# Layer-1 attention: value columns of four heads as the stationary operand, probabilities moved

## The chip, the core and the metric

The kernel runs on one core of a Trainium2 chip. The metric is the device time of one execution in microseconds. The core has TensorE (PE, with its weight loads shown apart as PEld), VectorE (DVE), ScalarE (ACT), GpSimd (POOL) and SyncE (SP), which here only issues transfers.

## What is computed

Two blocks over x of shape (2, 1024, 256): a cross attention of layer 0, a mixture of experts, a cross attention of layer 1 and a second feed-forward block. The change is in the third step. Its part of the reference:

```python
q = (queries @ Wq.T + bq).reshape(N, L, H, -1)        # N=2, L=1024, H=16 heads of 16
k = (keys @ Wk.T + bk).reshape(N, S, H, -1)           # S=77 context rows
v = (values @ Wv.T + bv).reshape(N, S, H, -1)
sm = jnp.einsum('nlhd,nshd->nlhs', q, k) / math.sqrt(D)
sm = jnp.where(causal_mask[None, :, None, :], -jnp.inf, sm)
sm = jax.nn.softmax(sm, axis=-1)
attn = jnp.einsum('nlhs,nshd->nlhd', sm, v)
return attn.reshape(N, L, H * D) @ Wo.T + bo
```

Only the first 77 tokens of a batch see a mask that cuts anything.

## The kernel before

Layer-1 attention (about 1440 to 1700 us of the profile) runs as a loop over 64 half heads, k = 0 to 63: two batches of 16 heads, and for each head two halves of 512 tokens. Each engine has its own program with its own copy of that loop, and dictionaries such as OUT_T, OUT_P, OUT_LN and R1V say at which k an engine does a side job. The order on an engine is the order in which the code is written; engines wait for one another by semaphores.

- Keys and queries are kept in split precision. Projected queries and keys are stored to DRAM and come back as stacks (QS, KS): for each head 49 rows with high and low parts and one row for the negated row maximum (NM). SP issues them (stack_queries1, stack_max1, stack_keys1). Chunk c = 0 holds heads 0 to 7 and c = 1 heads 8 to 15.
- Before the loop, bound matmuls with block keys KD give each token's maximum (max1); DVE reduces them, PE turns them, DVE negates them into NM, and SP sends them into QS. For the second batch all this happens inside the loop, at k = 17 to 28.
- scores1(k): one 512-column matmul gives 77 x 512 scores, in a PSUM bank of its own (two banks); for the first half one more adds the mask. PE runs it 3 half heads ahead.
- ACT takes the exponential into PT1 (a ring of four). The upper 16 bits of PT1 are the high part; the remainder PR1 is made by POOL, or by DVE where k is in R1V (k = 5, 7, 9, 11, then every fourth up to 31, then all odd ones).
- attend1(k): for each of four tiles of 128 tokens, four products with the tile's probabilities as stationary operand (128 columns) and the head's 16 value columns and a column of ones moved: 16 matmuls of 17 columns.
- norm1(n), on DVE, once per head: reciprocal of the sums (128 x 8) and a multiply (128 x 128) into Y, tokens on partitions.
- When a batch is done, its groups of 512 tokens are turned by PE (out_turn), rounded by ACT (round_out), the rest taken by DVE (rest_out), projected by PE (project_out1, 14 matmuls of 256 columns in each of two parts), added to X by DVE (add_out1) and normalised. Groups 0 and 1 run in the loop between k = 36 and 57, groups 2 and 3 behind it, one after the other. Then the router's matmuls (route) start.

The heart of the product before:

```python
for t in range(4):
    c = slice(t * P, t * P + P)
    mm = product(pv1[n % 2][:, 4 * a + t, :],
                 [(p[0:S, c], V1[v][0:S, b, h, :]) for p in (upper1(k), PR1[:, k % RING1, :]) for v in "hl"])
```

## Time and profile before

| | us |
|---|---|
| median of 3 runs (1809.47 to 1811.34) | 1811.26 |
| the profiled execution | 1816.01 |
| its span | 1814.2 |

| engine | busy us | share |
|---|---|---|
| PE | 1569.1 | 86% |
| PEld | 1287.9 | 71% |
| DVE | 1238.8 | 68% |
| ACT | 706.7 | 39% |
| POOL | 899.0 | 50% |

The mean granted clock of TensorE is 0.898 of full speed. A granted clock of 1.00 is 2.4 GHz and one of 0.50 is 1.2 GHz. A matmul's duration in the rows includes its way through the array and overlaps the next; the distance between two starts is its cost in a dense run. A line of the profile can be that of a helper: L1921 is the matmul inside product(), which attend1, the projections and the router all use.

### The profile page before, as it was taken

What the parts mean: (1) busy time and instruction counts of PE and PEld (TensorE: products, weight loads), DVE (VectorE), ACT (ScalarE), POOL (GpSimd) and SP (SyncE); (2) the same over time, 40 slices, a digit from 0 to 9 for tenths busy, and PEclk for the clock granted to TensorE, in tenths of its full rate; (3) what the DMA queues carried; (4) which work ended last, traced back from release to release, by engine and by line L of the source; (5) the groups of instructions that cost most, each with busy time, mean ns of one, the idle gap of its engine ahead of it and who ended that gap; (6) DMA issues with size and microseconds to landing.
All of it is one profiled execution on the core that took longest, in us unless ns stands there. A gap on an engine that the chain in (4) does not pass through costs nothing.

```text
span 1814.2 us, 44910 instructions
## 1 busy us (share of the span) xinstructions
PE 1569.1 (86%) x18034; PEld 1287.9 (71%) x18034; DVE 1238.8 (68%) x2503; ACT 706.7 (39%) x1312; POOL 899.0 (50%) x862
## 2 busy tenths in 40 slices
PE   1889999999999999999999975399988856898798
PEld 0777788777777778777877763299977834565587
DVE  8757777777777577777777775244488566455765
ACT  1334444444433454444444431155544404232122
POOL 3246555655564356565556651477655506221322
PEclk9899999999999999999999996599999955555699
DMA  9124424443432243344343416477776480600101
GB/s 216 37 62 125 97 71 112 109 105 85 103 96 64 69 100 85 96 108 106 84 106 93 112 37 227 178 260 258 251 243 209 157 137 1 116 3 1 36 12 36
DMA packets 83376, 199.60 MB, mean 110 GB/s; under 512 B 17739, under 2 KB 40835, under 8 KB 82788
## 3 DMA queue, kind: packets, MB, share of 16 engines
q1 hardware_dynamic: 79428, 186.47, 38.5%
q0 software_dynamic: 3744, 10.26, 1.5%
q8 instruction: 146, 2.39, 0.5%
q14 instruction: 58, 0.48, 0.1%
HBM read 104.46 MB, written 39.72 MB: 79 GB/s over the span
## 4 chain that ended last, share of the span: by engine, by line
PE 51%; DVE 20%; POOL 7%; issue 6%; ACT 6%; DMA 5%; DVEq 1%; ACTq 0%; SPq 0%; POOLq 0%
PE ps L1921 20%; PE ps L2020 9%; PE ps L1954 5%; PE ps L2000 5%; PE ps L2001 5%; DMA latf<-wexp 4%; POOL PR L869 3%; DVE PR L1420 3%; ACT hf L1178 2%; POOL wst L881 2%; DVE hf L1606 2%; ACT hs_h L1180 2%; DVE mxs L1354 2%; PE ps L2285 2%; DVE wtmp L1448 1%
## 5 line engine op out<-in xcount | busy, mean ns | idle before, releaser
L869 POOL TENSOR_TENSOR PR<-PT 128x512 f16<-128x512 f32 (+1 forms) x416 | 441.3, 1071 | 423.8 <-ACT PT L1093 423.1
L1093 ACT ACTIVATE PT<-ps 128x512 f32<-128x512 f32 (+1 forms) x576 | 324.1, 597 | 367.3 <-PE ps L2001 367.0
L2020 PE MATMUL ps<-V_h,PT 128*128 128x65 f16 (+1 forms) x2304 | 325.2, 197 | 26.8 <-DVE PR L1420 21.1
L2020 PE MATMUL ps<-V_l,PT 128*128 128x65 f16 (+1 forms) x2304 | 320.5, 195 | 0.0
L2020 PE MATMUL ps<-V_l,PR 128*128 128x65 f16 (+1 forms) x2304 | 318.8, 194 | 0.0
L2020 PE MATMUL ps<-V_h,PR 128*128 128x65 f16 (+1 forms) x2304 | 318.3, 194 | 0.0
L2020 PEld LDWEIGHTS ps<-V_h,PT 128*128 128x128 bf16 (+1 forms) x2304 | 227.0, 99 | 121.9 <-issue 48.2
L1354 DVE TENSOR_REDUCE mxs<-ps 128x1 f32<-128x736 f32 x256 | 235.3, 919 | 48.3 <-PE ps L1954 48.2
L2000 PE MATMUL ps<-QA,KA 128*128 128x512 f32 (+1 forms) x576 | 248.5, 431 | 5.5 <-DMA QB<-maxT 4.9
L2001 PE MATMUL ps<-QB,KB 65*128 65x512 f32 (+1 forms) x576 | 231.8, 402 | 0.0
L2020 PEld LDWEIGHTS ps<-V_l,PT 128*128 128x128 bf16 (+1 forms) x2304 | 228.9, 99 | 0.6
L2020 PEld LDWEIGHTS ps<-V_h,PR 128*128 128x128 f16 (+1 forms) x2304 | 227.7, 99 | 0.0
L2020 PEld LDWEIGHTS ps<-V_l,PR 128*128 128x128 f16 (+1 forms) x2304 | 226.3, 98 | 0.0
L1954 PE MATMUL ps<-KA,QA 128*128 128x368 f32 x768 | 198.3, 349 | 28.8 <-issue 17.5
L1352 DVE TENSOR_REDUCE mxs<-ps 128x1 f32<-128x368 f32 x256 | 137.2, 536 | 53.8 <-PE ps L1954 53.8
L1954 PEld LDWEIGHTS ps<-KA,QA 128*128 128x128 f32 x768 | 126.9, 190 | 48.8 <-issue 23.9
L1420 DVE TENSOR_TENSOR PR<-PT 128x512 f16<-128x512 f32 (+1 forms) x160 | 146.5, 931 | 10.3 <-ACT PT L1093 9.2
L937 POOL TENSOR_TENSOR hs_l<-hf,hs_h 128x512 f16<-128x512 f32 x92 | 110.7, 1208 | 62.4 <-ACT hs_h L1180 61.6
L1921 PE MATMUL ps<-xsp_h,wup 128*128 128x128 f16 x1472 | 132.9, 221 | 2.3 <-DVE xsp_l L1595 2.3
L2193 PE MATMUL ps<-wdn,hs_h 128*128 x736 | 123.8, 273 | 9.0 <-POOL hs_l L937 8.9
L1921 PE MATMUL ps<-xsp_l,wup 128*128 128x128 f16 x736 | 127.7, 221 | 0.0
L2000 PEld LDWEIGHTS ps<-QA,KA 128*128 128x128 f32 (+1 forms) x576 | 108.2, 188 | 26.6 <-issue 8.3
(351 smaller groups left out, 3670.3 us busy)
## 6 DMA issues: line engine op xcount, KB each, us to landing
wup<-wsplit SPq DMA_DIRECT2D x46, 1024.0 KB
QA<-Q_h SPq DMA_DIRECT2D x64, 256.0 KB, 4.6
latf<-wexp SPq DMA_DIRECT2D x32, 512.0 KB, 4.4
wsplit<-wst SPq DMA_DIRECT2D x32, 512.0 KB, 2.9
KA<-K_h SPq DMA_DIRECT2D x32, 275.5 KB, 3.1
KA<-K_l SPq DMA_DIRECT2D x32, 275.5 KB, 4.0
KB<-K_h SPq DMA_DIRECT2D x32, 275.5 KB, 5.4
QB<-Q_l SPq DMA_DIRECT2D x32, 256.0 KB, 5.5
```

The source lines that it names most:

```text
L869: nc.gpsimd.tensor_tensor(PR[0:m, s % RING, :], PT[0:m, s % RING, :], upper(s)[0:m], ALU.subtract).then_inc(s_rem_pool, 1)
L937: nc.gpsimd.tensor_tensor(hs["l"][:, j % 2, cols], hf[:, n % 3, :], hs["h"][:, j % 2, cols], ALU.subtract).then_inc(s_hlo, 1)
L1093: nc.scalar.activation(PT[0:m, s % RING, :], score_banks[s % 2][0:m], ACT.Exp, scale=HD ** -0.5).then_inc(s_exp, 1)
L1352: nc.vector.tensor_reduce(mxs[:, 0, t:t + 1], ps[:, 2, 0:MAXW], AX.X, ALU.max).then_inc(s_mxfree, 1)
L1354: nc.vector.tensor_reduce(mxs[:, 1, t:t + 1], ps[:, pair:pair + 2, 0:MAXW], AX.XY, ALU.max).then_inc(s_mxfree, 1)
L1420: nc.vector.tensor_tensor(PR[0:m, r % RING, :], PT[0:m, r % RING, :], upper(r)[0:m], ALU.subtract).then_inc(s_rem_dve, 1)
L1921: mm = nc.tensor.matmul(o, l, r, start=(k == 0), stop=(k == n - 1), **kw)
L1954: mm = nc.tensor.matmul(ps[:, 2 + i + (2 if two and a == 1 and t % 2 == 1 else 0), 0:MAXW], q, KA[h][:, MAXC[i]:MAXC[i] + MAXW], start=Tru ...
L2000: nc.tensor.matmul(o, KA[h][:, k], QA[h][:, q], start=True, stop=False)
L2001: nc.tensor.matmul(o, KB[h][0:HD + 1, k], QB[h][0:HD + 1, q], start=False, stop=True) \
L2020: mm = nc.tensor.matmul(pv_bank[:, q, :], p, v, start=(kt == 0 and q == 0 and k == 0), stop=(kt == KT - 1 and k == 3), skip_group_check=True)
L2193: mm = nc.tensor.matmul(out_banks[j % 2], hs[a][:, j % 2, f * P:f * P + P], down_weights(j, f // 4, b, slice(f % 4 * D, f % 4 * D + D)), s ...
```

## The change

The product is turned round. Four heads' value columns stand in a stationary operand of 128 columns: for head j of a chunk its 16 values are at columns 16j, ones for its sum are at the columns 64 away, and all else is zero. The probabilities, high part and remainder, are moved, 512 columns at a time, so one half head takes 4 matmuls of 512 columns (values high and low with each). Four heads add into one bank: values on 64 partitions, and each head's sum, replicated 16 times, on the other 64. The order of the half heads becomes: for a chunk and a group of four heads, the four heads of the first half, then the four of the second. norm1 runs once for four half heads, on 64 partitions x 512. Its output has channels on partitions, in Y's memory, so out_turn goes away; one rounding of 128 x 1024 and one remainder replace two each.

Scores, exponentials and remainders now work on all 128 rows: KS is cleared with a memset and its stationary is 128 columns wide. Both value arrays are cleared by POOL, with 16 small fills of ones. Query stacks are sent in quarters, and SP sends the maxima of the first batch before the second chunk's stacks. The output side jobs move: group 2 is now rounded at k = 60 and projected at k = 62 and 63, and only group 3 is projected behind the loop.

```diff
-        score1 = [ps[0:S, 3, :], ps[0:S, 4, :]]
-        pv1 = [ps[:, i, 0:TB * (D1 + 1)].rearrange("p (t d) -> p t d", t=TB) for i in (5, 2)]
+        score1 = [ps[:, 3, :], ps[:, 4, :]]
+        pv1 = [ps[:, 5, :], ps[:, 2, :]]
+        UNIT = 4
+
+        def half_head(k):
+            b, r = divmod(k, K1S // B)
+            u, i = divmod(r, UNIT)
+            c, g, a = u // 4, u // 2 % 2, u % 2
+            return b, c, g, a, i
+
+        def value_rows(g):
+            return slice(HD * g, HD * g + HD)
+
+        def sum_rows(g):
+            return slice(HD * (1 - g), HD * (1 - g) + HD)
+
+        def units_before(g):
+            return 8 * (g // 2) + 7 + g % 2
...
-        OUT_T, OUT_P, OUT_LN, OUT_XT = {36: 0, 43: 1}, {39: 0, 46: 1}, {42: 0, 49: 1}, {50: 0, 56: 1}
+        OUT_T, OUT_P, OUT_LN, OUT_XT = {29: 0, 35: 1, 60: 2}, {32: 0, 38: 1, 62: 2}, {35: 0, 41: 1}, {42: 0, 49: 1}
...
             stack_keys1(0)
-            for c in range(NC):
-                stack_queries1(0, c, 0)
+            for g in range(2):
+                stack_queries1(0, 0, g)
             sp.wait_ge(s_a1e, NM_JOB[0] + 2)
             for c in range(NC):
-                stack_max1(0, c, 0)
+                for g in range(2):
+                    stack_max1(0, c, g)
+            for g in range(2):
+                stack_queries1(0, 1, g)
             stack_keys1(1)
-            sp.wait_ge(s_comb, GR)
             sp.wait_ge(s_a1e, Q_DONE[1] - 1)
             store_queries1(1, 0)
             sp.wait_ge(s_a1e, Q_DONE[1])
             store_queries1(1, 1)
-            for c in range(NC):
-                stack_queries1(1, c, 0)
-            sp.wait_ge(s_sc1, 2 * (HC + 4))
-            for c in range(NC):
-                stack_queries1(1, c, 1)
+            sp.wait_ge(s_sc1, K1S // 4)
+            for g in range(2):
+                stack_queries1(1, 0, g)
             sp.wait_ge(s_a1e, NM_JOB[1] + 2)
-            for i in range(2):
-                for c in range(NC):
-                    stack_max1(1, c, i)
-
-            sp.wait_ge(s_a1e, OUT_JOB + 4 * GR)
+            for g in range(2):
+                stack_max1(1, 0, g)
+            sp.wait_ge(s_sc1, K1S // 2)
+            for g in range(2):
+                stack_max1(1, 1, g)
+            for g in range(2):
+                stack_queries1(1, 1, g)
...
-            nc.gpsimd.memset(V1["h"][:, :, :, D1:D1 + 1], 1.0).then_inc(s_l1c, 1)
-            nc.gpsimd.memset(V1["l"][:, :, :, D1:D1 + 1], 0.0).then_inc(s_l1c, 1)
+            for k in "hl":
+                nc.gpsimd.memset(V1[k][:], 0.0).then_inc(s_l1c, 1)
+            pool.wait_ge(s_l1c, 9)
+            for h in range(H1):
+                col = (D1 * h + HD) % P
+                nc.gpsimd.memset(V1["h"][0:S, :, h, col:col + D1], 1.0).then_inc(s_l1c, 1)
...
+                b, a = divmod(g, 2)
+                act.wait_ge(s_nm1, units_before(g))
+                act.wait_ge(s_a1, OUT_JOB + 2 * g)
+                nc.scalar.copy(A1T["h"], A1f[b][:, :, HALF * a:HALF * a + HALF]).then_inc(s_a1h, 1)
...
+            nc.vector.memset(KS[:].bitcast(F32), 0.0).then_inc(s_ones, 1)
+            dve.wait_ge(s_ones, 3)
             for c in range(NC):
-                nc.vector.memset(KS[HD * c + QM:HD * c + QM + 1].bitcast(F32), 1.0).then_inc(s_ones, 1)
+                nc.vector.memset(KS[HD * c + QM:HD * c + QM + 1, :, :, 0:S].bitcast(F32), 1.0).then_inc(s_ones, 1)
...
             def norm1(n):
-                b, h = divmod(n, H1)
-                dve.wait_ge(s_pv1, 2 * n + 2)
-                nc.vector.reciprocal(rs8[:, n % 2], pv1[n % 2][:, :, D1]).then_inc(s_rs1, 1)
-                dve.wait_ge(s_rs1, n + 1)
-                nc.vector.scalar_tensor_tensor(out=Y[:, TB * b:TB * b + TB, D1 * h:D1 * h + D1],
-                                               in0=pv1[n % 2][:, :, 0:D1], scalar=vs1[:, 1:2],
-                                               in1=rs8[:, n % 2].unsqueeze(2).to_broadcast([P, TB, D1]),
-                                               op0=ALU.mult, op1=ALU.mult).then_inc(s_nm1, 1)
+                b, c, g, a, _ = half_head(UNIT * n)
+                vr, sr, bank = value_rows(g), sum_rows(g), pv1[n % 2]
+                dve.wait_ge(s_pv1, UNIT * (n + 1))
+                link(dve, nc.vector.reciprocal(rec[vr], bank[sr]))
+                nc.vector.scalar_tensor_tensor(out=A1f[b][vr, c, HALF * a:HALF * a + HALF], in0=bank[vr], scalar=vs1[vr, 1:2],
+                                               in1=rec[vr], op0=ALU.mult, op1=ALU.mult).then_inc(s_nm1, 1)
 
             def rest_out(g):
-                for c in range(NC):
-                    rest_job(12 + NC * g + c, A1T["l"][:, c, :], tbank[(OUT_JOB + 4 * g + c) % 2], A1T["h"][:, c, :])
+                b, a = divmod(g, 2)
+                rest_job(12 + g, A1T["l"], A1f[b][:, :, HALF * a:HALF * a + HALF], A1T["h"])
...
-                    for b in range(B):
-                        ins = nc.vector.tensor_scalar(V1["h"][0:S, b, :, 0:D1], V1f[0:S, b], vs1[0:S, 0:1], None, ALU.mult)
+                    def values1(v, j):
+                        return v[0:S].rearrange("p b (c j) d -> p b c j d", c=NC)[:, :, :, j, :]
+
+                    for j in range(HC):
+                        ins = nc.vector.tensor_scalar(values1(V1["h"], j)[:, :, :, D1 * j:D1 * j + D1], values1(V1f, j),
+                                                      vs1[0:S, 0:1], None, ALU.mult)
                     link(dve, ins)
-                    for b in range(B):
-                        nc.vector.scalar_tensor_tensor(out=V1["l"][0:S, b, :, 0:D1], in0=V1f[0:S, b], scalar=vs1[0:S, 0:1],
-                                                       in1=V1["h"][0:S, b, :, 0:D1], op0=ALU.mult, op1=ALU.subtract) \
-                            .then_inc(s_v1, 1)
+                    for j in range(HC):
+                        nc.vector.scalar_tensor_tensor(out=values1(V1["l"], j)[:, :, :, D1 * j:D1 * j + D1], in0=values1(V1f, j),
+                                                       scalar=vs1[0:S, 0:1], in1=values1(V1["h"], j)[:, :, :, D1 * j:D1 * j + D1],
+                                                       op0=ALU.mult, op1=ALU.subtract).then_inc(s_v1, 1)
...
-            norm1(K1S // 2 - 1)
-            for g in range(GR // 2, GR):
-                rest_out(g)
-                for i in range(2):
-                    add_out1(g, i)
-                dve.wait_ge(s_a1e, OUT_JOB + 4 * g + 4)
-                normalise(dve, X, Y, 4 * g, 4, s_xn)
+            norm1(K1S // UNIT - 1)
+            add_out1(GR - 2, 1)
+            rest_out(GR - 1)
+            dve.wait_ge(s_a1e, OUT_JOB + 3 * GR - 2)
+            normalise(dve, X, Y, 4 * (GR - 2), 4, s_xn)
+            for i in range(2):
+                add_out1(GR - 1, i)
+            dve.wait_ge(s_a1e, OUT_JOB + 3 * GR)
+            normalise(dve, X, Y, 4 * (GR - 1), 4, s_xn)
...
             def scores1(k):
-                n, a = divmod(k, 2)
-                b, h = divmod(n, H1)
-                c = h // HC
+                b, c, g, a, i = half_head(k)
                 if k >= 2:
                     pe.wait_ge(s_ex1, k - 1)
-                o, j = score1[k % 2], h % HC
-                if a == 0 and h == 0:
+                if k % (K1S // B) == 0:
                     pe.wait_ge(s_ks[b], 16 * 6)
-                if a == 0 and (h % HC == 0 or (b > 0 and h % HC == 4)):
-                    pe.wait_ge(s_qs[b][c][h % HC // 4], 64)
-                slot = j if b == 0 else (HC + j) % QSLOTS
-                r = slice(HD * c, HD * c + QROWS)
-                mm = nc.tensor.matmul(o, KS[r, b, j, 0:S], QS[r, slot, HALF * a:HALF * a + HALF], start=True, stop=(a == 1))
+                if a == 0 and i == 0:
+                    pe.wait_ge(s_qs[b][c][g], 64)
+                o, j, r = score1[k % 2], 4 * g + i, slice(HD * c, HD * c + QROWS)
+                mm = nc.tensor.matmul(o, KS[r, b, j, :], QS[r, j, HALF * a:HALF * a + HALF], start=True, stop=(a == 1))
                 if a == 0:
-                    mm = nc.tensor.matmul(o[:, 0:P], ident_r[0:S, 0:S], mask[0:S, 1, :], start=False, stop=True)
+                    mm = nc.tensor.matmul(o[:, 0:P], ident_r[0:S, :], mask[0:S, :], start=False, stop=True)
                 mm.then_inc(s_sc1, 1)
 
             def attend1(k):
-                n, a = divmod(k, 2)
-                b, h = divmod(n, H1)
-                if a == 0 and n >= 2:
+                n = k // UNIT
+                b, c, g, a, i = half_head(k)
+                if i == 0 and n >= 2:
                     pe.wait_ge(s_nm1, n - 1)
                 if k in R1V:
                     pe.wait_ge(s_r1v, R1V.index(k) + 1)
                 else:
                     pe.wait_ge(s_r1p, k + 1 - sum(v <= k for v in R1V))
-                for t in range(4):
-                    c = slice(t * P, t * P + P)
-                    mm = product(pv1[n % 2][:, 4 * a + t, :],
-                                 [(p[0:S, c], V1[v][0:S, b, h, :]) for p in (upper1(k), PR1[:, k % RING1, :]) for v in "hl"])
+                h = HC * c + 4 * g + i
+                for m, (v, p) in enumerate((v, p) for v in "hl" for p in (upper1(k), PR1[:, k % RING1, :])):
+                    mm = nc.tensor.matmul(pv1[n % 2], V1[v][:, b, h, :], p, start=(i == 0 and m == 0),
+                                          stop=(i == UNIT - 1 and m == 3))
                 mm.then_inc(s_pv1, 1)
-
-            def out_turn(g):
-
-                pe.wait_ge(s_nm1, H1 * (g // 2 + 1))
-                for c in range(NC):
-                    bk = job(OUT_JOB + 4 * g + c)
-                    for t in range(4):
-                        mm = nc.tensor.transpose(bk[:, t * P:t * P + P], Y[:, 4 * g + t, c * P:c * P + P], ident[:])
...
-                if k in OUT_T:
-                    out_turn(OUT_T[k])
                 for i in range(2):
                     if k - i in OUT_P:
                         project_out1(OUT_P[k - i], i)
                 if k in OUT_XT:
                     transposes(2, OUT_XT[k])
-            for g in range(GR // 2, GR):
-                out_turn(g)
-                for i in range(2):
-                    project_out1(g, i)
-            for g in range(GR // 2, GR):
-                transposes(2, g)
-
-
-            pe.wait_ge(s_a1e, OUT_JOB + 4 * GR)
+            transposes(2, GR - 2)
+            for i in range(2):
+                project_out1(GR - 1, i)
+            transposes(2, GR - 1)
```

## Rows read from the trace of the kernel before

**Rows 1.** Page: busy sums, and granted TensorE clock in 40 slices

```profile
PE 1569.1 (86%) x18034; PEld 1287.9 (71%) x18034; DVE 1238.8 (68%) x2503; ACT 706.7 (39%) x1312; POOL 899.0 (50%) x862
...
PEclk9899999999999999999999996599999955555699
```

**Rows 2.** Busy us (count) per engine, granted clock, DMA share, GB/s

```profile
1520.00:1530.00 10.00, 4.86 (x61) 3.81 (x60) 8.97 (x24) 3.68 (x7) 6.93 (x7) 0.50 0.00 1
...
1550.00:1560.00 10.00, 9.23 (x68) 6.53 (x68) 3.61 (x7) 2.56 (x4) 1.05 (x2) 0.66 0.26 105
...
1640.00:1650.00 10.00, 10.00 (x116) 6.59 (x114) 7.64 (x17) 5.10 (x9) 3.40 (x4) 0.50 0.01 2
1700.00:1710.00 10.00, 9.33 (x44) 4.63 (x43) 10.00 (x15) 3.87 (x6) 7.91 (x3) 0.82 0.00 0
```

**Rows 3.** PE in order of time, two steps: start us, us, operation

```profile
1501.97 0.71 PE L2285 MATMUL ps<-QS,KS 49*77 49x512 f32 x1
1502.61 0.20 PE L1921 MATMUL ps<-V_h,PT 77*128 77x17 f16 x1
...
1503.14 0.71 PE L2285 MATMUL ps<-QS,KS 49*77 49x512 f32 x1
...
1504.54 0.71 PE L2285 MATMUL ps<-QS,KS 49*77 49x512 f32 x1
```

**Rows 4.** PE in order of time, 512-column f32r matmuls at either clock

```profile
1545.26 0.63 PE L1921 MATMUL ps<-XT_l,wa_h 128*128 128x512 f32 x1
1545.69 0.63 PE L1921 MATMUL ps<-XT_h,wa_l 128*128 128x512 f32 x1
...
1711.18 0.40 PE L1921 MATMUL ps<-XT_h,diag_l 128*128 128x512 f32 x1
1711.42 0.39 PE L1921 MATMUL ps<-XT_l,diag_h 128*128 128x512 f32 x1
```

**Rows 5.** DVE groups by shape, 1490 to 1720: busy us, mean ns, idle before

```profile
L1725 DVE SCALAR_TENSOR_TENSOR Y<-ps,vs,rs 128x128 f32<-128x128 f32 x32 | 11.2, 351 | 1.1
...
L1723 DVE RECIPROCAL rs<-ps 128x8 f32<-128x8 f32 x32 | 6.5, 204 | 33.6 <-PE ps L1921 33.3
...
L1661 DVE SCALAR_TENSOR_TENSOR A<-ps,bqk,Q_h 128x512 fp32r<-128x512 f32 x4 | 3.0, 744 | 2.4 <-ACT Q_h L1144 2.4
...
L1852 DVE RECIPROCAL logits<-logits 128x128 f32<-128x128 f32 x1 | 1.0, 953 | 0.0
```

**Rows 6.** DVE's remainders, line 1801: duration ns min/median/max

```profile
L1801 DVE TENSOR_TENSOR PR<-PT x25: 676/1187/3317, 1509.5 to 1657.2; 77x512 f16<-77x512 f32 x25
```

**Rows 7.** Chain that ended last, both transfers of maxima: start us, us, what

```profile
1483.56 13.07 DMA QS<-NM
...
1586.62 2.17 DMA QS<-NM
1588.92 0.68 PE ps L2285
```

**Rows 8.** Two microseconds of the first wait for maxima, columns as above

```profile
1486.00:1488.00 2.00, 0.00 (x0) 0.00 (x0) 1.97 (x7) 0.00 (x0) 0.00 (x0) 0.50 1.10 119
```

**Rows 9.** DVE and POOL in order of time ahead of the loop

```profile
1440.10 1.10 DVE L1704 MEMSET KS<- 1x1248 f32 x1 [0.31 <-issue]
...
1443.85 0.31 POOL L977 MEMSET mask_f<- 128x256 f32 x1
...
1467.69 0.38 POOL L1007 PARTITION_ALL_REDUCE vb<-vb  x1 [11.28 <-DVE vb L1766]
```

**Rows 10.** End of the loop and tail: DVE, chain, and the router's first matmul

```profile
1658.59 0.21 DVE L1723 RECIPROCAL rs<-ps 128x8 f32<-128x8 f32 x1 [0.70 <-PE ps L1921]
...
1662.65 9.25 PE ps L1921 x32
...
1678.88 9.25 PE ps L1921 x32
...
1697.94 0.59 PE L1921 MATMUL ps<-XT_h,wr_h 128*8 128x512 f32 x1 [1.45 <-issue]
```

More of the change, by code:

```diff
@@ L70 @@
 XJ = 2 * GR
-QSLOTS = HC + 4
 QH, QL, QM, QH2, QROWS = 0, D1, 2 * D1, 2 * D1 + 1, 3 * D1 + 1
@@ L226, in sb2 @@
             return st2.enter_context(nc.sbuf_tensor(name, shape, dt))
-        mask_f = sb2("mask_f", [P, 2, P])
-        mask = sb2("mask", [P, 2, P], F32R)
+        mask = sb2("mask", [P, P], F32R)
         mask4 = sb2("mask4", [P, HC // 2, SP], F32R)
@@ L374, in program @@
         s_q1d = [[sem(f"layer1_queries{b}_{c}_stored") for c in range(NC)] for b in range(B)]
-        s_qs = [[[sem(f"layer1_query_stack{b}_{c}_{i}_loaded") for i in range(1 + b)] for c in range(NC)] for b in range(B)]
+        s_qs = [[[sem(f"layer1_query_stack{b}_{c}_{i}_loaded") for i in range(2)] for c in range(NC)] for b in range(B)]
         s_vb, s_vbr = sem("layer1_value_bounds"), sem("layer1_value_bound_ready")
@@ L1226, in _ @@
                     act.wait_ge(s_pv1, k - RING1 + 1)
-                nc.scalar.activation(PT1[0:S, k % RING1, :], score1[k % 2], ACT.Exp, scale=D1 ** -0.5).then_inc(s_ex1, 1)
+                nc.scalar.activation(PT1[:, k % RING1, :], score1[k % 2], ACT.Exp, scale=D1 ** -0.5).then_inc(s_ex1, 1)
                 if k in APPLY_AT:
@@ L1715, in max1_rows @@
                     for c in range(NC):
-                        dve.wait_ge(s_qs[0][c][0], 64)
+                        for g in range(2):
+                            dve.wait_ge(s_qs[0][c][g], 64)
                 nc.vector.tensor_scalar(NM[:, HALF * half:HALF * half + HALF], tbank[j % 2][0:H1], -1.0, None,
@@ L1795, in _ @@
             for k in range(K1S):
-                if k % 2 == 0 and k > 0:
-                    norm1(k // 2 - 1)
+                if k % UNIT == 0 and k > 0:
+                    norm1(k // UNIT - 1)
                 r = k + 1
@@ L2368, in _ @@
                     transposes(2, OUT_XT[k])
[L2369 to L2377 removed]
+            transposes(2, GR - 2)
+            for i in range(2):
+                project_out1(GR - 1, i)
+            transposes(2, GR - 1)
+            pe.wait_ge(s_a1e, OUT_JOB + 3 * GR)
             route(2, 1, LT1)
```

89 lines of the change are left out of this document (43 added, 46 removed).

## The prediction

> **What bounds the kernel now.** I read the page's slices first: PE is busy in 86% of the span, and its granted clock is at half over the stretch from about 1450 to 1700 us [rows 1]. That stretch is layer-1 attention. The rows of ten microseconds then show two regimes [rows 2]: around 1525 PE is busy for half of the time, because DVE, ACT and POOL are finishing layer norms; from 1590 on PE is busy without a break, and still at 1.2 GHz. The clock is up only in part of the stretches from 1550 and from 1700, behind runs of 512-column matmuls. So "busy" alone doesn't bring 2.4 GHz here: the matmuls of 17 columns that fill PE now don't do it.
>
> One step of the loop (scores of a half head, then its product with the values) is read from PE's order of time [rows 3]: 1501.97 to 1503.14 is a step without the mask, 1.17 us; 1503.14 to 1504.54 one with it, 1.40 us; mean 1.285. The scores take 0.64 of it, the 16 small matmuls 0.43 and about 0.10 goes until the next scores. DVE's part is small now: per half pair a reciprocal of 0.20 and a multiply of 0.35 [rows 5], and every second remainder. It becomes the question below.
>
> **The value products.** Removed: 16 matmuls of 17 columns per half head, 0.43 us. Added: 4 matmuls of 512 columns. No row shows a 512-column f16 matmul. The bounds are from below the columns alone at the clock, from above the f32r matmul of the same width, which starts every 0.43 us at 1.2 GHz and every 0.23 to 0.24 at 2.4 GHz [rows 4]; 512 columns at 1.2 GHz are 0.427 us, so at half clock both ends meet. I take 4 x 0.43 = 1.71 us at half clock and 0.93 at full (0.85 the lower end). A step becomes 0.64 + 1.71 + 0.10 + half of the mask's 0.23 = 2.55 us at half clock, and about 1.4 at full (scores 0.23 plus an exposed 0.1 to 0.2, as at half clock they cost 0.21 over their columns). Against 1.285 that is +1.27 us in 64 steps, +81 us, if the clock stays; near nothing if it is always up. Wider stationaries (128 instead of 77 columns of keys and mask) lie under that; 0 to 0.1 us each.
>
> The page "TensorE: Matmul & The Clock Gate" of the Trainium skill, section "Back-to-back issue gap", prices matmuls by moved columns, with a floor of about 25 ns for small ones. That speaks against this change: 16 floors are swapped for 2048 columns. The 0.43 us for 16 agree with it.
>
> **Normalisation on DVE, the term that is easy to miss.** Before, a reciprocal works on 8 numbers per partition; after, on 64 partitions x 512, since the sums come out replicated. The reciprocal rows give its slope: 204 ns for 8, 953 ns for 128, so 6.24 ns per number [rows 5], and 953 + 384 x 6.24 = 3.35 us for 512. The multiply behind it is nearest to the 128x512 scalar-tensor-tensor of 0.74 us [rows 5]. One normalisation is 4.1 us, once in four half heads, where two of 0.6 stood: 16 x 4.1 = 66 us of DVE in place of 19.
>
> The page "VectorE: DVE Perf Modes", section "First, the fixed hardware budget", of the Trainium skill says reciprocal is an iterated divide with a repeat count of 8. A cheap one, at the 1.3 ns per number of the undisturbed remainder [rows 6], would be 0.7 us and the wait below would be gone; the slope of the rows sides with the page.
>
> Who waits: behind the normalisation in DVE's queue stands the remainder of the second half head of the next unit wherever DVE makes it (units at k = 4 and 8, and all from k = 32 on). It costs 0.68 us undisturbed [rows 6]. PE needs it 0.1 + 4.1 + 0.68 + 0.1 = 5.0 us after the last product of the old unit. As cover PE has two scores and one product: 0.64 + 0.10 + 1.71 + 0.64 + mask 0.2 = 3.3 at half clock, 1.75 at full. It waits 1.7 or 3.2 us. A unit of four is then 5.0 + 1.71 + 2 x 2.45 + 0.2 = 11.8 us at half clock and 5.0 + 0.93 + 2 x 1.33 + 0.1 = 8.7 at full, where it was 5.1.
>
> **Start of the loop.** The negated maxima wait 13.07 us behind query stacks that fill the queues; the second batch's same transfer takes 2.17 [rows 7]. The change sends the maxima ahead of the second chunk's stacks: three transfers of 8 heads x 16 rows x 4 KB (1.5 MB), 13 us at the 119 GB/s of that moment [rows 8]. So the wait falls to some 2.2 us: -10.9. DVE adds ahead of it: a memset of 2048 numbers (0.88 ns each by the 1248-number memset of 1.10 us, 1.8 us [rows 9]) and eight small splits of the values in place of two (+1.3), less half a mask copy (-0.8): +2.3. POOL clears two arrays of 4096 f16 numbers; by 0.31 us for 256 [rows 9] 3.5 us each, plus 16 small fills, some 11 us, in a pause of POOL of 11.3 us [rows 9], cover nearly used up: 0 to +1. Sum -8.6.
>
> **Steps 0 to 28** (1496.8 to 1588.9, 92 us). PE's own work is 29 x 1.285 = 37, projections 24 x 0.43 = 10, transposes 4, bound matmuls about 9 (36 x 312/512 x 0.43), turns 2: 62; it waits for 30. After at half clock: 62 + 29 x 1.27 = 99, plus normalisation waits at k = 4 and 8 (3.4), at k = 20 and 24, where max reductions stand behind it (4), and at k = 28, where the second maxima's copy does (4): 110, +18. With the clock up from the 512-column projections on, twelve steps and half of the projections are cheaper by 19: 91, -1. I take +8.
>
> **Steps 29 to 63** (1588.9 to 1658.6, 69.7 us [rows 7, 10]). Half clock: 3 x 2.55 + 8 x 11.8 + 5 half-group projections at 9.25 / 2 [rows 10] = 23.1, of which 1.7 fills a wait, + transposes 2 x 1.9: 127, +58. Full: 4.2 + 69.6 + 10 - 3 + 2 = 83, +13. The new products should bring the clock up, as the 512-column runs do in [rows 2]; a wait of 3.2 us in every unit should let it fall again, as waits do around 1525. I take the middle, 105: +35.4. The output turns (L2311, 2 x 1.9) are left out already.
>
> **Tail** (1658.6 to the router's first matmul at 1697.9, 39.3 us [rows 10]). Group 2 moves into the loop except for its addition and norm. After: 4.1 normalisation (the projection of 4.6 runs beside it), 0.7 addition, 1.3 remainder of the output, 5.2 norm of group 2, for which PE's queue waits before it may project, 2 transposes, 9.25 projection, 9.8 as before from there: 32.9. -6.4; with a fast clock -11.
>
> **Sum:** -8.6 + 8 + 35.4 - 6.4 = +28.4 us. The profiled execution takes 1816.0 with a span of 1814.2, 0.3% over the runs' median of 1811.3; on the median it is 1840.
>
> **Rivals.** (1) The clock never comes up in the loop: -8.6 + 18 + 58 - 6.4 = +61, 1872 us. For it: PE is busy throughout at 1640 and stays at half clock. Against: those are 17-column matmuls. (2) Other side: the waits of 3.2 us are too short to drop the clock, which stays at 2.4 GHz from about k = 17: -8.6 - 1 + 13 - 11 = -8, 1803 us. It decides from about 80% of steps at full clock. The same page's table of the two clock states has sustained work release the clock and a longer idle throttle it; by that rule this rival would be the result, at the same 1803. The row at 1640 argues against the first half of it. (3) The wide reciprocal is cheap (0.7 us): no waits, dense PE, fast clock: 4 + 8 x 5.6 + 10 + 2 = 61 for steps 29 to 63, -9; with -8.6, -5 and -14 elsewhere, 1775 us. Against it the two reciprocal rows lie on one line. (4) The maxima still queue behind the first chunk's stacks: +5 on the forecast, inside its chance.
>
> **Chances.** Forecast 0.60 (own range 1820 to 1862), rival 1 0.16, rival 2 0.14, rival 3 0.05, within a few us of the old time by chance of the mix 0.05. A measurement tells apart about 0.2%, 3.6 us. Faster: 0.11 + 0.04 = 0.15; same 0.04; slower 0.81. The range goes from rival 2 to rival 1: 1803 to 1872.
>
> **What would show it.** Right: the products as 128x512 rows every 0.43 or 0.22 us; a DVE reciprocal 64x512 of 3.3 us; PE idle 1.7 to 3.2 us per unit from k = 32 with DVE's remainder as releaser; a clock row between 0.5 and 1.0 there; the first scores at about 1488; the tail 33 us. Wrong: a reciprocal under 1.5 us, or a clock row that is 0.5 or 1.0 throughout.

## The result and the profile after

| | before | after |
|---|---|---|
| median of 4 runs each, us | 1811.30 | 1857.41 |
| lowest to highest | 1809.47 to 1813.44 | 1853.71 to 1858.49 |
| span of the profiled execution | 1814.2 | 1855.8 |
| mean granted clock | 0.898 | 0.918 |

The ratio is 1.0252, 95% interval 1.0236 to 1.0267. The change makes the kernel slower by 46 us, at a higher mean clock; the forecast was 1840 us. The page's busy sums, and the slices of PE and of its clock, which answer to [rows 1]:

```profile
PE 1589.1 (86%) x17223; PEld 1263.6 (68%) x17234; DVE 1294.9 (70%) x2480; ACT 705.3 (38%) x1308; POOL 907.4 (49%) x878
...
PE   1899999999999999999999952999989578786698
...
PEclk9899999999999999999999975999999658777699
```

DVE's sum is up by 56 us, PE's by 20. The clock is no longer flat at half over the loop. Three points cut the time up: the first scores, the first scores of the second batch (k = 32, issued at step 29), and the last value product. In order of time on PE, then the router's first matmul:

```profile
1491.57 0.76 PE L2311 MATMUL ps<-QS,KS 49*128 49x512 f32 x1 [3.13 <-DMA QS<-NM]
1601.69 0.76 PE L2311 MATMUL ps<-QS,KS 49*128 49x512 f32 x1 [6.23 <-DMA QS<-NM]
1706.89 0.38 PE L2327 MATMUL ps<-PR,V_l 128*128 128x512 f16 x1
1739.49 0.59 PE L1951 MATMUL ps<-XT_h,wr_h 128*8 128x512 f32 x1 [1.45 <-issue]
```

Before, the first two and the last stood at 1496.77, 1588.92 and 1697.94, and the last product, just ahead of the reciprocal of [rows 10], at 1658.37. So steps 0 to 28 take 110.1 us in place of 92.2, steps 29 to 63 take 105.2 in place of 69.5, and the tail 32.6 in place of 39.6. I call the first two stretches A and B below. The sum -5.2 + 18.0 + 35.7 - 7.0 is 41.6 us, the difference of the spans.

DVE's groups between 1480 and 1720 (columns as in [rows 5]) show what was added:

```profile
L1748 DVE RECIPROCAL rec<-ps 64x512 f32<-64x512 f32 x16 | 53.7, 3355 | 36.2 <-PE ps L2327 36.0
L1827 DVE TENSOR_TENSOR PR<-PT 128x512 f16<-128x512 f32 x25 | 20.7, 839 | 0.2
L1749 DVE SCALAR_TENSOR_TENSOR Y<-ps,vs,rec 64x512 f32<-64x512 f32 x16 | 12.0, 750 | 0.6
```

One unit in DVE's order of time, and PE's next product in its own:

```profile
1672.40 3.36 DVE L1748 RECIPROCAL rec<-ps 64x512 f32<-64x512 f32 x1 [1.61 <-PE ps L2327]
1675.79 0.74 DVE L1749 SCALAR_TENSOR_TENSOR Y<-ps,vs,rec 64x512 f32<-64x512 f32 x1
1676.46 1.28 DVE L1827 TENSOR_TENSOR PR<-PT 128x512 f16<-128x512 f32 x2
```
```profile
1677.19 0.61 PE L2327 MATMUL ps<-PT,V_h 128*128 128x512 bf16 x1 [2.73 <-DVE PR L1827]
```

The unit's last product ends at 1672.3, DVE inverts and multiplies until 1676.5, only then makes the remainder, and PE has stood for 2.73 us. The ten-microsecond rows (columns as in [rows 2]) show the clock moving between its two levels:

```profile
1640.00:1650.00 10.00, 9.57 (x43) 4.50 (x43) 9.76 (x19) 3.96 (x7) 3.46 (x3) 1.00 0.00 1
1660.00:1670.00 10.00, 8.37 (x23) 3.86 (x22) 6.94 (x5) 2.30 (x5) 2.41 (x2) 0.52 0.00 0
1680.00:1690.00 10.00, 8.50 (x18) 2.96 (x20) 5.13 (x4) 2.39 (x4) 1.95 (x2) 0.50 0.01 2
```

### The profile page after: what moved, and what is told of

Same layout as the page of the kernel before. It is cut to its first block, busy times and chain, and to the rows that moved or that the text cites. A ratio compares the mean times of both kernels' runs of the same rounds, so it can differ in the third digit from the quotient of the medians.

```text
span 1855.8 us, 43284 instructions
## 1 busy us (share of the span) xinstructions
PE 1589.1 (86%) x17223; PEld 1263.6 (68%) x17234; DVE 1294.9 (70%) x2480; ACT 705.3 (38%) x1308; POOL 907.4 (49%) x878
## 4 chain that ended last, share of the span: by engine, by line
PE 50%; DVE 24%; issue 6%; POOL 6%; ACT 6%; DMA 4%; DVEq 1%; ACTq 0%; SPq 0%; POOLq 0%
PE ps L1951 17%; PE ps L2050 10%; PE ps L1984 6%; PE ps L2030 5%; PE ps L2031 5%; DVE PR L1441 3%; DMA latf<-wexp 3%; PE ps L2327 3%; POOL PR L887 3%; DVE rec L1748 3%; ACT hf L1200 2%; DVE hf L1627 2%; POOL wst L899 2%; ACT hs_h L1202 2%; DVE mxs L1376 2%
## 5 line engine op out<-in xcount | busy, mean ns | idle before, releaser
L1376 DVE TENSOR_REDUCE mxs<-ps 128x1 f32<-128x736 f32 x256 | 234.9, 917 | 48.4 <-PE ps L1984 48.3
L1374 DVE TENSOR_REDUCE mxs<-ps 128x1 f32<-128x368 f32 x256 | 136.9, 535 | 53.7 <-PE ps L1984 53.7
```

What stands on the lines that cost most here:

```text
L1374: nc.vector.tensor_reduce(mxs[:, 0, t:t + 1], ps[:, 2, 0:MAXW], AX.X, ALU.max).then_inc(s_mxfree, 1)
L1376: nc.vector.tensor_reduce(mxs[:, 1, t:t + 1], ps[:, pair:pair + 2, 0:MAXW], AX.XY, ALU.max).then_inc(s_mxfree, 1)
```

## The experiments

Stretches A and B, in us, from the same three rows of each profile. The stage does not start at the same time in every execution: the first memset of the key stack stood at 1440.10 before [rows 9], at 1436.35 after, and between 1436.16 and 1441.10 in all profiles. So differences of up to 5 us in the column of the first scores mean little, and the stretches are the firmer numbers. The kernel after was timed once, at another time than the rest, each of which was timed beside the kernel before (medians of 1809.5 to 1811.4); the difference of two medians below can be off by 2 us for that.

| kernel | median | ratio to before, 95% | first scores | A | B |
|---|---|---|---|---|---|
| before | 1811 | 1 | 1496.8 | 92.2 | 69.5 |
| after | 1857.4 | 1.0236 to 1.0267 | 1491.6 | 110.1 | 105.2 |
| clear_later | 1851.9 | 1.0210 to 1.0246 | 1486.2 | 110.0 | 105.2 |
| late_norm | 1836.1 | 1.0124 to 1.0175 | 1490.9 | 102.9 | 91.0 |
| late_and_clear | 1826.7 | 1.0051 to 1.0096 | 1484.7 | 97.7 | 94.0 |
| cheap_recip | 1815.1 | 1.0014 to 1.0047 | 1489.9 | 87.3 | 72.6 |
| cheap_late_clear | 1798.3 | 0.9916 to 0.9952 | 1486.6 | 89.9 | 71.8 |
| invert_on_act | 1829.5 | 1.0082 to 1.0144 | 1484.1 | 97.3 | 96.2 |
| half_products | 1838.1 | 1.0109 to 1.0176 | 1495.2 | 104.4 | 87.4 |
| double_scores | 1831.6 | 1.0093 to 1.0132 | 1486.4 | 111.3 | 85.3 |
| before_with_recip | 1836.8 | 1.0119 to 1.0171 | 1491.2 | 103.5 | 83.2 |
| before_recip_last | 1832.4 | 1.0102 to 1.0138 | 1493.4 | 95.5 | 82.5 |
| order_alone | 1803.3 | 0.9936 to 0.9976 | 1487.6 | 95.4 | 69.5 |
| order_again | 1802.8 | 0.9931 to 0.9969 | 1482.3 | 94.1 | 69.5 |

**Its place in DVE's queue.** The edit:

```diff
-                if k % UNIT == 0 and k > 0:
-                    norm1(k // UNIT - 1)
                 r = k + 1
                 if r in R1V:
                     ...
+                if k % UNIT == 0 and k > 0:
+                    norm1(k // UNIT - 1)
```

> The changed kernel, with one edit: where a unit of four half heads ends, DVE first makes the remainder of half head k+1 and only then the reciprocal (3.35 us) and the multiply (0.74 us). Theory A (PE's wait behind the wide reciprocal, and the clock that falls with it, are what steps 29 to 63 cost): PE's wait for DVE's remainder falls from 1.3 to 3.8 us per unit to under 0.7, the granted clock of steps 29 to 63 stays up for more than three quarters of them, that stretch shrinks from 105.6 us to 70 to 85, and the kernel comes to 1825 to 1838 us. Theory B (the moved columns at a half clock are the cost, the wait is incidental): the stretch stays above 98 us, the kernel above 1850.

Measured: 1836.1 us, B 91.0. From 1600 to 1700 PE waits for a remainder once, where it did six times (us in total, times, longest); a seventh wait of the changed kernel, of 3.55 us, ends at 1700.20. After, then this kernel:

```profile
PE ps L2327 <- DVE PR L1827: 12.5, 6, 3.8
```
```profile
PE ps L2327 <- DVE PR L1825: 3.2, 1, 3.2
```

Theory A holds in direction and size of the total (-21 us), but not in its picture of the clock: the row of ten microseconds from 1650 is at 0.58 and the mean over B is 0.78, against 0.73 in the changed kernel. B lost 14 us, not 20 to 35, and A, which the expectation left out, another 7.

**The reciprocal itself.** The edit, in norm1:

```diff
-                link(dve, nc.vector.reciprocal(rec[vr], bank[sr]))
+                link(dve, nc.vector.tensor_copy(rec[vr], bank[sr]))
```

> The changed kernel with a copy of the same 64x512 numbers in place of the reciprocal, so the attention is multiplied by the sums and not divided by them; all else stays, the order too. Theory A: the copy takes 0.4 to 0.8 us in place of 3.35, a normalisation 1.3 in place of 4.1; PE's waits for DVE's remainder nearly vanish, steps 0 to 28 lose 6 to 10 us (DVE is full there) and steps 29 to 63 about 25 to 35: 1815 to 1827 us. Theory B (columns at a half clock): no more than the 16 x 2.6 us of DVE in waits that were exposed and no clock, at most -10: 1847 or more.

Measured: 1815.1 us, 42 less. DVE's group of the copy:

```profile
L1748 DVE COPY rec<-ps 64x512 f32<-64x512 f32 x16 | 11.0, 689 | 21.6 <-PE ps L2327 21.4
```

DVE works 42.7 us less (53.7 - 11.0), and by the medians the kernel is 42.3 us shorter (40.5, if each is taken against the kernel before timed beside it): 40 to 42 of the 46 us hang on this one instruction, and Theory B is out. The profiled execution took 1797.4 us, at a mean clock of 0.937; ten of the twelve took 1809 to 1822, at 0.925 to 0.933. So its A of 87.3 and B of 72.6 are those of an execution in which the clock was up for longer than in most, and the 42.3 is that of the medians. In it A lost 23 us, where the expectation had 6 to 10.

**The same amount of reciprocals in the kernel before.** Nothing of the change is in it. DVE inverts 64x512 constants out of SBUF, as two instructions of 1.745 us:

```diff
+                if k % 4 == 0 and k > 0:
+                    dve.wait_ge(s_pv1, k)
+                    for i in range(2):
+                        link(dve, nc.vector.reciprocal(mask_f[0:HD].rearrange("p a n -> p (a n)"), gbs[0:HD, i, :]))
                 if k % 2 == 0 and k > 0:
                     norm1(k // 2 - 1)
```

> The kernel before, with nothing but the wide reciprocal added: at every fourth half head, behind the products it would belong to, DVE inverts 64x512 constants into a tile that nothing reads, as two of 64x256 (3.5 us together), ahead of its normalisation and its remainder. Theory A (the reciprocal ahead of the remainder costs by itself, whatever the products are): the cover is 2.2 us here and PE waits about 2.9 us in each of ten units whose remainder DVE makes, and 0 to 3.5 us in the five others, where DVE is full: +27 to +45 us, 1837 to 1855. Rival J (it is the combination with the moved columns and their clock that costs): +10 or less, under 1820 us.

Measured: 1836.8 us, +25.4, just under Theory A's range of +27 to +45 and far over Rival J's. PE's waits between 1480 and 1700, before and with the reciprocal:

```profile
PE ps L1921 <- DVE PR L1801: 9.4, 4, 5.1
```
```profile
PE ps L1925 <- DVE PR L1805: 31.1, 10, 8.5
```

Placed last in the step's list:

> The kernel before with the idle reciprocal of 64x512 numbers added at every fourth half head, but last in DVE's list of its step, behind the remainder. In this kernel a unit of four half heads takes 5.1 us and DVE then has 3.6 + 4 x 0.28 + 2 x 0.68 = 6.1 us or more in it. Theory N (DVE's sum per unit is over PE's, so the place in the list moves the wait and does not remove it): +12 to +22 us over before, 1823 to 1833. Theory A alone (only the place ahead of the remainder costs): +8 or less.

Measured: 1832.4 us, +21.4, in Theory N's range: A is back to 95.5, but B stays at 82.5. The theory's reason, that DVE's work per unit is more than PE's, is not what the trace shows: in B DVE is busy for 67.9 of the 82.5 us. PE goes on waiting for remainders all the same, 22.9 us in 9 waits where it was 31.1 in 10. So the place in the queue gives back 4 us here and 21 in the changed kernel; why it is so much less here was not tested.

**The columns.** Each half head moves 2048 columns in its value products. The edit that halves them, on late_norm, and the one that adds 512 per half head, on late_and_clear:

```diff
-                for m, (v, p) in enumerate((v, p) for v in "hl" for p in (upper1(k), PR1[:, k % RING1, :])):
+                for m, (v, p) in enumerate((v, p) for v in "h" for p in (upper1(k), PR1[:, k % RING1, :])):
```
```diff
+                nc.tensor.matmul(o, KS[r, b, j, :], QS[r, j, HALF * a:HALF * a + HALF], start=True, stop=True)
                 mm = nc.tensor.matmul(o, KS[r, b, j, :], QS[r, j, HALF * a:HALF * a + HALF], start=True, stop=(a == 1))
```

> The kernel with the remainder ahead of the normalisation (1836 us), with two of the four value products left out (those with the low part of the values), so that the output lacks that part: 1024 moved columns per half head in place of 2048. It prices the columns by themselves. Theory H (in the loop PE's columns are what is left to bound the time): 2 x 0.22 us less per half head at the full clock and 2 x 0.43 at half, 64 x 0.44 to 0.86 = 28 to 55 us, half of them in waits: -20 to -40, 1796 to 1816 us. Rival I (DVE's 5.5 us for a unit bound it, PE only fills): 0 to -10, 1826 to 1836 us.

Measured: 1838.1 us, no less than the 1836.1 with all four products, and 2 over Rival I's range. A and B together are 2 us shorter, and the first scores come 4 us later, in a part of the program that the edit does not touch (see the start, below). Rival I is near in time for a reason that is only half right, as PE's rows show:

```profile
1620.34 0.61 PE L2327 MATMUL ps<-PT,V_h 128*128 128x512 bf16 x1
1620.75 0.63 PE L2327 MATMUL ps<-PR,V_h 128*128 128x512 f16 x1
1621.31 0.79 PE L2311 MATMUL ps<-QS,KS 49*128 49x512 f32 x1
1622.03 0.61 PE L2327 MATMUL ps<-PT,V_h 128*128 128x512 bf16 x1
```
```profile
1620.00:1630.00 10.00, 9.90 (x24) 4.42 (x24) 8.76 (x17) 3.32 (x5) 3.56 (x3) 0.50 0.00 0
1630.00:1640.00 10.00, 9.75 (x31) 6.63 (x30) 7.20 (x9) 1.20 (x2) 1.04 (x1) 0.50 0.00 0
```

A step is 1.69 us with two products (1620.34 to 1622.03), PE is busy without a break, and the clock is granted at 0.50. With four products at the upper level, 1.00, a step was 1.42 (the changed kernel, below). The columns that were taken away were paid for by the clock: its mean over B is 0.58, against 0.78.

> The kernel with the clears behind the mask copies and the normalisation last (1827 us), with each score matmul of 512 columns issued twice into the same bank, the second in place of the first, so the result is the same and PE has one more 512-column matmul per half head, six with the mask in place of five. It is the mirror of the run with half of the products. Theory K (PE's columns and its clock trade off: what is added in columns comes back by a clock that is up for longer): -5 to +8 us, 1822 to 1835, with a higher mean clock over the loop. Theory H (PE's columns add at whatever clock): 64 x 0.21 to 0.43 = +14 to +27 us, 1841 to 1854.

Measured: 1831.6 us, 5 more. The total is Theory K's, but the stretches go opposite ways. B is 9 us shorter, at a mean clock of 0.91 against 0.73: there K holds. A is 14 us longer, at 0.68 against 0.79: more columns, and a lower clock. K doesn't say why, and no run here does. The ten microseconds from 1610 without the added matmuls, then two rows with them:

```profile
1610.00:1620.00 10.00, 10.00 (x29) 5.46 (x27) 6.40 (x8) 1.19 (x2) 1.83 (x1) 0.50 0.01 2
```
```profile
1520.00:1530.00 10.00, 10.00 (x26) 3.99 (x24) 3.09 (x13) 3.75 (x7) 4.29 (x5) 0.50 0.00 0
...
1610.00:1620.00 10.00, 10.00 (x49) 5.79 (x48) 5.10 (x16) 2.64 (x4) 1.81 (x2) 1.00 0.11 14
```

PE is fully busy in both rows from 1610, and has the lower level in one and the upper in the other. With the added matmuls it is fully busy in all five rows from 1490 to 1540 too, and at the lower level in each of them.

**The start.** POOL clears the value arrays while DVE has to copy the masks. The changed kernel, DVE and then POOL in order of time:

```profile
1451.35 2.60 DVE L1766 TENSOR_TENSOR KD<-K_h,hmask 128x624 fp32r<-128x624 f32 x2
1453.87 9.29 DVE L1776 CAST mask<-mask_f 128x128 fp32r<-128x128 f32 x1
1455.10 8.23 DVE L1777 CAST mask<-mask_f 128x312 fp32r<-128x312 f32 x1
```
```profile
1451.60 3.49 POOL L983 TENSOR_TENSOR wa_l<-wa_raw,wa_h 128x512 fp32r<-128x512 f32 x2 [5.41 <-ACT wa_h L1225]
...
1455.12 3.51 POOL L1008 MEMSET V_h<- 128x4096 f16 x1
1458.57 3.51 POOL L1008 MEMSET V_l<- 128x4096 f16 x1
1462.03 1.02 POOL L1012 MEMSET V_h<- 77x32 f16 x16
```

The edit, in POOL's program:

```diff
+            pool.wait_ge(s_ones, 7)
             for k in "hl":
                 nc.gpsimd.memset(V1[k][:], 0.0).then_inc(s_l1c, 1)
```

> The changed kernel, with one edit: POOL waits for DVE's two mask copies before it clears the two arrays of values. Theory A (the clears hold up DVE's copies at the start): the two mask copies fall from 9.3 and 8.2 us to about 1.0 and 0.3, the negated maxima are there some 8 us sooner, 1857 becomes 1848 to 1852. Rival D (the clears only move the loss: DVE's copy of the values or the bounds wait for them later, or the next copies stall in the same way): within 3 us of 1857.

```profile
1455.56 1.40 DVE L1777 CAST mask<-mask_f 128x128 fp32r<-128x128 f32 x1
1456.79 0.33 DVE L1778 CAST mask<-mask_f 128x312 fp32r<-128x312 f32 x1
```

Measured: 1851.9 us, -5.5, all of it ahead of the loop: A and B are the same to 0.1 us, and the first scores start 5.4 earlier, where 8 was expected. Theory A holds, by the trace: the two ratios' intervals overlap. The Trainium skill, page "SBUF — State Buffer", section "SBUF: two separate sides", says that VectorE and GpSimd share one pair of ports, and that an instruction of GpSimd, or one of VectorE of the kinds that use the pair, has it for its whole length while the other engine blocks. The rows agree. They add that the loser can wait for more than one instruction: here the copy is held from 1453.87, with the subtraction still running, until POOL's back-to-back instructions are done at 1463.

How long it is held changes from one execution to the next. Four kept traces have the same program up to the first scores. In this one and in half_products the two copies take 9.3 and 8.2 us; in cheap_recip they take 4.84 and 3.78 and in late_norm 1.30 and 3.75, because DVE comes in ahead of POOL's second clear. From the first memset of the key stack to the first scores it is 55.2 and 57.7 us in the first two, 51.7 in both of the others, and 47.8 to 48.3 in all five kernels with the clears moved. So the collision costs 3.4 to 9.9 us.

**All that was found, together.** Clears behind the mask copies, and the normalisation behind the max reductions and the second maxima's copy too:

> The changed kernel with three edits: POOL clears the value arrays behind DVE's mask copies, and the normalisation stands last in DVE's list of its step, behind the remainder, the max reductions and the copy of the second batch's negated maxima (in the run with the remainder first it stood ahead of those two, and PE still waited 3.37 us for a reduction and 6.23 us for the second maxima). Theory A (every place where the wide reciprocal stands ahead of something that PE wants costs its 4 us): -21 for the remainder, -5.5 for the clears, -4 to -8 for steps 20 to 28: 1822 to 1828 us. Rival F (DVE is full in steps 0 to 28, so that an order within it and an earlier start bring nothing there): 1830 to 1836 us.

Measured: 1826.7 us, ratio 1.0073. A is 97.7, 5.2 under late_norm's: Theory A. The second maxima's wait is 3.06 us in place of 6.23. PE still waits twice for a reduction, 4.1 and 4.0 us, now at the step behind, and 4.6 for a remainder at 1507, where the block keys stand ahead of it.

> The kernel with the clears behind the mask copies and the normalisation last in DVE's list (1827 us), with the reciprocal replaced by a copy of the same 64x512 numbers, so that the output is not divided by the sums. It leaves the new layout of the products without the reciprocal. Theory A (DVE's 3.35 us cost also where they stand last, since DVE is busy for seven to nine tenths of the loop): 1806 to 1814 us. Rival M (standing last, the reciprocal is hidden, and what is left over the kernel before is the price of the products and their clock): 1820 us or more.

Measured: 1798.3 us, 8 below the range of Theory A. Standing last, the reciprocal still costs 28 us. Against cheap_recip, the order and the clears take another 17 us off the median and leave A and B as they were in its profiled execution: all four executions now lie within 3 us, as its quickest did. The clock stays up (the row from 1600 to 1610):

```profile
1600.00:1610.00 10.00, 10.00 (x53) 6.40 (x52) 8.48 (x14) 2.01 (x4) 3.79 (x3) 1.00 0.01 2
```

**The sums inverted on ACT.** The sums are inverted as exp(-log(sum)): ACT does it at the end of the following unit's exponentials, and DVE only multiplies:

```diff
+                act.wait_ge(s_pv1, UNIT * (n + 1))
+                act.wait_ge(s_nm1, n)
+                nc.scalar.activation(rec[vr], pv1[n % 2][sr], ACT.Ln).then_inc(s_ones, 1)
+                act.wait_ge(s_ones, 7 + 2 * n + 1)
+                nc.scalar.activation(rec[vr], rec[vr], ACT.Exp, scale=-1.0).then_inc(s_ones, 1)
```

> As the last kernel, but the sums are inverted on ACT, by a logarithm and an exponential of 64x512 numbers each (about 0.6 us each by ACT's exponential of 128x512), and DVE only multiplies (0.74 us), one step later. Nothing of the computation is left out. Theory A (DVE's time for the reciprocal is the loss): at least the gain of the cheap copy, 1857 - 42 - 5 = 1800 to 1812 us. Rival G (ACT has to change its function tables twice in four half heads, and the exponentials of the scores stand behind that): PE waits for ACT, 1825 us or more.

```profile
1626.09 1.28 ACT L1249 ACT_TABLE_LOAD   x1
...
1627.38 0.59 ACT L1249 ACTIVATE rec<-ps 64x512 f32<-64x512 f32 x1
...
1627.99 1.28 ACT L1251 ACT_TABLE_LOAD   x1
...
1629.28 0.63 ACT L1251 ACTIVATE rec<-rec 64x512 f32<-64x512 f32 x1
1629.93 0.60 ACT L1260 ACTIVATE PT<-ps 128x512 f32<-128x512 f32 x1
```

Measured: 1829.5 us, in Rival G's range. ACT is away from the scores for 3.8 us in each unit, nearly the 4.1 of DVE before. PE's own waits for ACT come to only 3.7 us (3 waits), and it waits 6.9 us for remainders, which DVE makes from ACT's exponentials; how much of that is ACT's doing was not separated. The Trainium skill, page "ScalarE: Activation LUTs", section "Table sets: the hidden batching unit", says that one table set holds both functions and one load serves them. The trace disagrees: a load stands ahead of each of the 16 logarithms and the 16 exponentials behind them, at 1.28 us.

**The order of the transfers alone.** The kernel before with one part of the change:

```diff
-            for c in range(NC):
-                stack_queries1(0, c, 0)
+            stack_queries1(0, 0, 0)
             sp.wait_ge(s_a1e, NM_JOB[0] + 2)
             for c in range(NC):
                 stack_max1(0, c, 0)
+            stack_queries1(0, 1, 0)
```

> The kernel before, with the one part of the change that concerns the maxima: SP sends the rows of negated maxima ahead of the stacks of the second chunk's queries. Theory A (the transfer's wait of 13.07 us is what holds the first scores): the wait falls to 2 to 4 us, the first scores start 9 to 11 us sooner and the kernel takes 1800 to 1804 us. Rival E (the first 28 steps are bound by DVE's queue, so that an earlier start is given back there): 1807 to 1811 us, with more waits of PE in steps 0 to 28.

> The kernel before with the maxima ahead of the second chunk's query stacks, once more and in more rounds, since it was under both kernels by 0.4%: 1800 to 1807 us, ratio 0.994 to 0.998. If the first figure was the chance of its chip and hour, the ratio includes 1.000.

Both waits for maxima in order_again, and then the second of them in the kernel before:

```profile
1482.33 0.68 PE L2285 MATMUL ps<-QS,KS 49*77 49x512 f32 x1 [3.90 <-DMA QS<-NM]
...
1576.46 0.68 PE L2285 MATMUL ps<-QS,KS 49*77 49x512 f32 x1 [5.07 <-DMA QS<-NM]
```
```profile
1588.92 0.68 PE L2285 MATMUL ps<-QS,KS 49*77 49x512 f32 x1 [3.05 <-DMA QS<-NM]
```

Measured: 1803.3 us (ratio 0.9936 to 0.9976) and 1802.8 us (0.9931 to 0.9969). The first wait is down to 3.90 us, where a transfer of 13.07 stood [rows 7]; stretch A grows by 2 to 3, and the second maxima are waited for 5.07 us where it was 3.05. Against the kernel before timed beside them the medians are 6.2 and 8.2 us lower, so Theory A, with 2 to 4 of its 10 us given back. This version beats both kernels, by the only part of the change that was tried by itself in the old kernel.

## Why the prediction came out as it did

The direction, the mechanism and the largest term were right; the sum was 17 us short. Of that, 10.0 us lie in steps 0 to 28 and 3.4 in the start; the last 4.5 are in no term: the forecast was built on a profiled execution that stood 4.7 us over its kernel's median, and the profile after stands at its own.

| term | forecast | measured |
|---|---|---|
| start | -8.6 | -5.2, of which 3.75 is an earlier start of the stage in that execution |
| steps 0 to 28 | +8 | +18.0 |
| steps 29 to 63 | +35.4 | +35.7 |
| tail | -6.4 | -7.0 |

- **Reciprocal and multiply.** 3.35 and 0.74 us forecast, 3.355 and 0.750 measured; 66 us of DVE forecast, 65.7 measured. The line through two small shapes held at four times their size.
- **Value products.** A start every 0.43 us at the lower clock and every 0.22 at the upper one, as [rows 4] had it. The f16 and bf16 matmuls follow the lower end of the bounds. A step at the lower level takes 2.54 us without the mask (scores at 1526.38 and 1528.92) and 2.86 with it (1604.52 and 1607.38), where the forecast had 2.45 and 2.68. At the upper level it is 1.42 us:

```profile
1670.87 0.50 PE L2311 MATMUL ps<-QS,KS 49*128 49x512 f32 x1
...
1672.29 0.50 PE L2311 MATMUL ps<-QS,KS 49*128 49x512 f32 x1
```

- **Start: a term that failed.** "POOL clears two arrays ... in a pause of POOL ...: 0 to +1". The duration of 3.5 us was right, though the row that it names, 0.31 us for 256 numbers, gives 5.0 by proportion; the pause was there. What was not asked is who else is hurt by a busy POOL. It was DVE, whose copies waited 8 us. From the first memset to the first scores the stage lost only 1.5 us (56.7 to 55.2), where -8.6 was forecast; with the clears moved it is 48.1 in clear_later, which is -8.6. The other terms of that sum were sound, then, though the agreement to 0.1 us is partly chance: 54.0 to 56.7 are measured with the old start. The transfer's own gain was there: the wait ended at 3.1 us, and by itself in the old kernel this order is worth 6 to 8.
- **Steps 0 to 28: the step that failed most.** The forecast of +8 is a middle between the lower clock (110 us) and the upper (91), with 3.4 + 4 + 4 us of waits. Measured was 110.1 at a mean clock of 0.73, so it isn't the clock of the first case. The stretch before and after (columns as in [rows 2]):

```profile
1496.77:1588.92 92.15, 69.75 (x596) 44.62 (x597) 50.96 (x105) 31.04 (x56) 40.17 (x35) 0.52 0.31 58
```
```profile
1491.57:1601.69 110.12, 83.60 (x243) 37.67 (x249) 78.19 (x106) 31.29 (x56) 40.38 (x35) 0.73 0.32 51
```

  The forecast let the new columns fill all of the time for which PE had waited (30 us by its sum, 22.4 by the row) and put 11.4 us of waits on top. PE's busy time grew by 14 us, not by 37, since the clock was up for part of it; but its idle time did not shrink, it is 26.5 us. The three kinds of waits that the forecast lists came to 7.0 us (remainders), 7.3 (reductions) and 6.2 (second maxima), and two that it doesn't list, for DVE's part of the transposed activations (XT_l), to 5.0. DVE is full in the first thirty microseconds (9.76, 9.76 and 9.83 of 10 busy from 1490 on), though not over the whole stretch (78.2 of 110.1). There the norm, the block keys (4.34 us for two, where one takes 0.80 undisturbed) and the remainder (2.65, undisturbed 0.68) form one queue, beside a busy POOL:

```profile
1504.17 3.36 DVE L1748 RECIPROCAL rec<-ps 64x512 f32<-64x512 f32 x1
1507.57 0.74 DVE L1749 SCALAR_TENSOR_TENSOR Y<-ps,vs,rec 64x512 f32<-64x512 f32 x1
1508.23 0.95 DVE L1827 TENSOR_TENSOR PR<-PT 128x512 f16<-128x512 f32 x1
1509.11 4.34 DVE L1766 TENSOR_TENSOR KD<-K_h,hmask 128x624 fp32r<-128x624 f32 x2
1513.37 2.65 DVE L1827 TENSOR_TENSOR PR<-PT 128x512 f16<-128x512 f32 x1
```

  Seven normalisations fall into this stretch (23.5 us of reciprocals, where 14 of 0.204 were 2.9). A sum of waits at five places leaves out that a queue that is full for a time passes every us on. With the cheap copy the stretch took 87.3 in a quick execution; with the normalisation last and the clears moved it is 97.7 with the reciprocal and 89.9 with the copy.
- **Steps 29 to 63.** 105 forecast, 105.2 measured, by units of 8.7 to 11.8 us. The waits were forecast at 1.7 to 3.2 us in each of eight units, 14 to 26 us; measured are seven, of 0.3 to 3.8 us, 16.0 in all. The rest is the clock: 0.73 in the mean, 0.50 in whole rows of ten microseconds. The middle was a choice, and it is partly chance that it lies so near. That nearly all of the difference to the kernel before hangs on the reciprocal was argued rightly: with the copy the stretch is 72.6, and 71.8 in cheap_late_clear, whose four executions agree.
- **Tail.** 32.6 us, with a forecast of 32.9 (the terms that it lists add up to 32.4, with 2 us for the transposes); 9.05 us of wait for the norm of group 2 stands in it.
- **Rivals.** (1), half clock throughout at 1872, is out by the clock row; 1857 lies between it and the forecast for other reasons. (2), 1803, had 91 and 83 us for the two stretches; only without the reciprocal was it reached (89.9 and 71.8 in cheap_late_clear). Its point of decision, four fifths of the steps at the upper clock, was not: a mean clock of 0.73 in both stretches is the upper level for under half of the time, by an estimate from the two levels. (3) is the same finding read backwards: at 0.69 us for the first of the two instructions the kernel takes 1815.1 (1797.4 profiled), not 1775; B is 72.6 at best, where 61 was put, and the start is what it is above. (4), maxima that still queue, is out: 3.13 us.

What the change is worth without the reciprocal: cheap_late_clear is 4.5 us under the old kernel with the new order of transfers alone (1798.3 and 1802.8, timed beside the same runs of the kernel before). By their profiles its tail is 8.6 us shorter (30.9 against 39.6), A and B together are 1.9 us shorter (161.7 against 163.6), and its first scores come 4.3 us later. So the new products are near 0: a step without the mask takes 2.54 us at the lower level and 1.42 at the upper, against 1.17 before, and of the 24.2 us for which PE stood idle in A (order_again) 13.3 are left. That is argued from a comparison of two kernels that differ in more than the products, and not from one edit.

## What to carry to other kernels

A layout that makes results come out replicated also replicates the work behind it: cost every elementwise instruction by its new size per partition, a reciprocal above all, and look at what stands behind it in its engine's queue. Here, with that engine busy for 140 of 215 us of the loop, moving the instruction behind the remainder won half of it back (21 of 42 us), and a cheap copy in its place nearly all; in the old kernel with the same reciprocals the move won only 4 of 25. Before an idle engine is given a long clear, see what its neighbour copies at that moment; and don't expect fewer matmul columns to be faster, nor more to be slower, until the granted clock of the new mix has been read.
